# A mixture-of-experts kernel: the experts' multiplications in whole fp32 on row halves of TensorE, instead of high and low parts

## The chip, the cores and the metric

One core of a Trainium2 chip runs the kernel. The metric is the time of one execution in device microseconds (us); three runs of the kernel before gave 1051.89, 1052.32 and 1053.75 us, median 1052.32. Everything is fp32 on the outside.

## What is computed

The input x is 64 images of 64 channels and 16x16 pixels. First comes a normalisation over the channels, two quantised 3x3 convolutions with batch normalisation, and residual sums. The result is read as 16384 tokens of 64 channels, and each token goes through its best two of eight experts:

```python
logits = flat @ router_w.T
topk_probs, topk_idx = jax.lax.top_k(jax.nn.softmax(logits, axis=-1), 2)
gates = ...                                   # the two probabilities, normalised to a sum of 1
h1 = jnp.einsum('nc,ehc->neh', flat, w1)      # c = 64, h = 682
h3 = jnp.einsum('nc,ehc->neh', flat, w3)
y = jnp.einsum('neh,ech->nec', silu(h1) * h3, w2)
out = jnp.einsum('ne,nec->nc', gates, y)
```

The kernel computes only the two experts that a token is sent to: 32768 rows of 64 numbers.

## The kernel before, in words

**Stages.** Normalisation and the first convolution (to about 124 us of the span), then the second convolution with the routing (to about 265), then the experts, 68 tiles of up to 512 rows (to about 996), then the gated sum of each token's two results and the store. Each engine has its own program; order between them comes from semaphores alone.

**Routing, in eight pairs of stripes** (`pairs`, `route`). A stripe is 1024 tokens. For each pair, VectorE finds the two experts and the place of each token's row in a DRAM table `expert_rows` in which every expert has a region. GpSimd (POOL) copies a stripe's rows and places into its own buffers (`stage`, lines 556 and 557) and writes them to the table by 16 indirect DMAs of 128 rows (line 563). In `route(p)` the weights of expert p are also made ready: VectorE splits them into a high part (rounded to fp32r) and a low part (`high`, `low`, lines 970 to 983), TensorE turns eleven blocks of 128x128 (`stack_weights`, line 1341) and six pieces of w2 (lines 1348, 1349), ScalarE copies them out of PSUM (lines 702 to 707), and SyncE (SP) writes them to DRAM. `stack_weights(p)` stands on TensorE ahead of the transposes and logits of the next pair and of the position sums of this one.

**Tiles.** A tile is 512 rows of one expert; 56 of them (NF) are full, the other 12 hold 256 rows each of two experts ("two"). `tiles` gives the order on all engines. Per tile:
- SP loads the rows (`load_rows`) and the weights (`load_weights`: w1 and w3 stacked, 704 KB, and w2, 192 KB), two tiles ahead, when the buffers of the tile two before are free.
- VectorE `split` (lines 1126 to 1145): where each result row goes, and the rows' high and low parts side by side in `hl`.
- TensorE `turn` (line 1384): four transposes to PSUM; ScalarE `copy_xT` (lines 732 to 735) copies them to two tiles, [high; low] and [low; high] over the 128 partitions, in three instructions.
- TensorE `up` (line 1405): the 682 hidden columns are six blocks (KT), five of 128 and one of 42. A block takes two fp32r multiplications for h1 and two for h3, each over all 128 rows of the array (64 channels, high and low). In the last block the 42 columns of h1 and the 42 of h3 lie in one stationary tile. That makes 22 multiplications of 512 columns in a full tile.
- ScalarE `silu` (line 726), VectorE `hidden` (line 1157, the product), with PSUM banks in threes.
- TensorE `down` (line 1420): whole fp32 multiplications, whose stationary operand is 64 columns wide. Blocks k and k+1 go to the two column halves of the array: `y_ps[h:h + 64]`, h = 0 or 64. The last block has 42 rows. A whole fp32 multiplication leaves two records in the trace, an fp32r one leaves one.
- ScalarE `copy_y` (line 740), TensorE `rows_out` (line 1432, four transposes), VectorE `rows_out` (lines 1164 and 1165), and POOL `scatter_y` (line 583): four indirect DMAs of 128 rows into `result_rows`.

**What orders the work around it.** TensorE's tile j is written out by hand: turn(j+1), up 2, up 3, down 0, up 4, rows_out(j-1), up 5, down 2, up 0 and up 1 of tile j+1, down 4. VectorE's `rows_out(j)` waits until POOL's results of tile j-2 are stored (`y_out`), since there are two buffers. POOL's own order is fixed too:

```python
            def four_tiles(j, s, u):
                stage(s, u)
                for i in range(4):
                    scatter(u, i // 2, range(i % 2 * G, i % 2 * G + G))
                    scatter_y(j + i, i % 2)
```

So POOL writes six stripes alone, then one of the other ten stripes per four tiles: in tiles 0 to 39 it issues four indirect DMAs of rows and four of results per tile. In tiles 40 to 47 it issues two of pad rows (line 594) and four of results, in tiles 48 to 67 four of results alone.

Of the kernel before, what the change touches and what calls it, by code (L numbers as in the profile page):

```python
# [15 lines left out]
ALU = mybir.AluOpType  # L16
# [13 lines left out]
def conv_moe_kernel(nc, x, gamma1, beta1, w1, gamma2, beta2, w2, pat, router_w, ew1, ew2, ew3, out):  # L30
# [29 lines left out]
    WST = (2 * HT + 1) * 128  # L60
    LV = len(SNAPS)
    TAIL3 = 64
# [9 lines left out]
    with ExitStack() as ctx:  # L72
# [90 lines left out]
        wr = sb("w13_rows", [128, 2, HT, C])  # L163
        wt = sb("w13_tail", [128, C])
        wr2 = sb("w2_rows", [C, HID])
        wsp = sb("w13_split", [128, 2 * HT + 1, 2, C], F32R)
        wstk = sb("w13_stacked", [128, WST], F32R)
# [3 lines left out]
        wbuf = [[sb(f"w13_{u}", [128, WST], F32R)[:, :] for u in range(2)]]  # L171
# [3 lines left out]
        wbuf.append([wsp[:, :, :, :].rearrange("p t d c -> p (t d c)"), wstk[:, :]])  # L175
# [20 lines left out]
        hbuf = [carve(T) for u in range(4)]  # L196
# [5 lines left out]
        xT = [[sb(f"xT_{p}_{u}", [128, T], F32R) for u in range(2)] for p in ("hi_lo", "lo_hi")]  # L202
# [55 lines left out]
        w_zero = sem("w_zeroed")  # L258
        ws_rdy = sem("w_split_ready")
# [111 lines left out]
        def _(sp):  # L371
# [21 lines left out]
            sp.wait_ge(w_zero, 1)  # L393
            def weights_in(e):
                for k, w in enumerate((ew1, ew3)):
                    we = w.rearrange("e h c -> e (h c)")
                    sp.dma_start(wr[:, k, :, :].rearrange("p t c -> p (t c)"),
                                 we[bass.ds(e, 1), 0:HT * 128 * C].rearrange("a (p n) -> (a p) n", p=128)
                                 ).then_inc(w_in, 16)
                    sp.dma_start(wt[TAIL3 * k:TAIL3 * k + HR, :],  # L400
                                 we[bass.ds(e, 1), HT * 128 * C:HID * C].rearrange("a (p n) -> (a p) n", p=HR)
                                 ).then_inc(w_in, 16)
# [4 lines left out]
            def weights_out(e):  # L407
                sp.dma_start(wsc[bass.ds(e * 128, 128), :], wstk[:].bitcast(F32)).then_inc(w_out, 16)
# [4 lines left out]
            with sp.Fori(0, E - 1) as e:  # L413
                sp.wait_ge(ws_rdy, 2 * e + 2)
                weights_in(e + 1)
                sp.wait_ge(wt_sb, 4 * e + 4)
                weights2_in(e + 1)
                weights_out(e)
            sp.wait_ge(wt_sb, 4 * E)
# [21 lines left out]
            def load_weights(j, u, two=0, first=False):  # L441
                for i in range(1 + two):
                    at = tmap[0:1, 2 + two, bass.ds(2 * j - 2 * NF + i if two else j, 1)]
                    exp = sp.value_load(at, min_val=0, max_val=(E - 1) * 128)
                    if not first and i == 0:
                        sp.wait_ge(h1_rdy, KT * j - KT)
                    sp.dma_start(wbuf[i][u].bitcast(F32), wsc[bass.ds(exp, 128), :]).then_inc(wt_in[i][u], 16)
# [193 lines left out]
        def _(act):  # L641
# [48 lines left out]
            def route(p, first=False, last=0):  # L690
# [8 lines left out]
                for b in range(3):  # L699
                    n = min(512, WST - 512 * b)  # L700
                    act.wait_ge(wt_ps, 4 * p + b + 1)
                    nc.scalar.activation(wstk[:, 512 * b:512 * b + n], w_bank(b)[:, 0:n],
                                         ACT.Copy).then_inc(wt_sb, 1)
                act.wait_ge(wt_ps, 4 * p + 4)
                nc.scalar.activation(w2s[:, 0:HT, :].rearrange("p k c -> p (k c)"), w_bank(3)[:, 0:HT * C],
                                     ACT.Copy)
                nc.scalar.activation(w2s[0:HR, HT, :], w_bank(3)[0:HR, HT * C:KT * C],
# [20 lines left out]
            def copy_xT(j, u, part):  # L728

                if part == 0:  # L730
                    act.wait_ge(xt_rdy, j + 1)
                    nc.scalar.activation(xT[0][u][:], turn_ps[:], ACT.Copy)  # L732
                    nc.scalar.activation(xT[1][u][0:C, :], turn_ps[C:2 * C, :], ACT.Copy)  # L733
                else:
                    nc.scalar.activation(xT[1][u][C:2 * C, :], turn_ps[0:C, :], ACT.Copy).then_inc(xt_sb, 1)  # L735
# [6 lines left out]
            def tile(j, u, two, first=False, last=0):  # L742
                if not first:
                    copy_y(j - 1, 1 - u)
                if last != 1:
                    copy_xT(j + 1, 1 - u, 0)
                silu(j, 2)
                if last != 1:
                    copy_xT(j + 1, 1 - u, 1)
                for k in range(3, KT):  # L750
                    silu(j, k)
                if last != 1:
                    silu(j + 1, 0)
                    silu(j + 1, 1)

            copy_xT(0, 0, 0)
            copy_xT(0, 0, 1)
            silu(0, 0)
            silu(0, 1)
# [15 lines left out]
        def _(dve):  # L775
# [34 lines left out]
            V.memset(wt[:], 0.0)  # L810
            V.memset(w2s[:], 0.0).then_inc(w_zero, 1)
# [63 lines left out]
            pipelined(dve, spread, norm, NP)  # L875

# [86 lines left out]
            def route(p, first=False, last=0):  # L963
                c = r_chain.begin(p, 21)
                wideof = lambda a, n: a.unsqueeze(2).broadcast_to([128, a.shape[1], n])
                wr_ = wr[:].rearrange("p k t c -> p (k t) c")
# [3 lines left out]

                def high():
                    dve.wait_ge(w_in, 64 * p + 64)
                    V.tensor_copy(wsp[:, 0:2 * HT, 0, :], wr_)
                    V.tensor_copy(wsp[:, 2 * HT, 0, :], wt[:]).then_inc(ws_rdy, 1)

                def low(n):
                    def work():
                        dve.wait_ge(ws_rdy, 2 * p + 1)
                        a = slice(4 * n, min(4 * n + 4, 2 * HT))
                        ins = V.tensor_tensor(wsp[:, a, 1, :], wr_[:, a], wsp[:, a, 0, :].bitcast(F32), ALU.subtract)  # L980
                        if 4 * n + 4 >= 2 * HT:
                            V.tensor_tensor(wsp[:, 2 * HT, 1, :], wt[:], wsp[:, 2 * HT, 0, :].bitcast(F32), ALU.subtract
                                            ).then_inc(ws_rdy, 1)
                    return work
# [14 lines left out]
                assert 2 * HT <= 12  # L999

# [492 lines left out]
```

## Time and profile before

| | us |
|---|---|
| median of three runs | 1052.32 |
| runs | 1051.89 to 1053.75 |
| span of the profiled execution | 1053.6 |
| TensorE busy / VectorE / ScalarE / POOL | 932.6 / 627.8 / 500.6 / 611.6 |
| first `up` to the end of the last tile | 269.7 to about 996 |

The span runs from the first to the last instruction; no other time of the profiled execution is shown, and the span is 1.3 us over the median. Busy means that at least one instruction of the engine was under way. Ends of multiplications are modelled and overlap, so TensorE can look busy throughout while it streams less than it could; the distance from one start to the next is the better measure. PE is TensorE's multiplication, PEld its load of the stationary operand, DVE VectorE, ACT ScalarE.

### The profile page before, as it was taken

To read this page: it belongs to the slowest core of one execution; us is meant where nothing else is said; L and a number is where in the kernel's file an instruction comes from. 1 tells how busy PE (TensorE), PEld (TensorE's weight loads), DVE (VectorE), ACT (ScalarE), POOL (GpSimd) and SP (SyncE) were. 2 spreads that over 40 slices of the span, in tenths; PEclk is the share of its full clock that TensorE was granted. 3 is DMA by queue.
4 is the path that set the end of the run, shared out by engine and by line. 5 is a ranking of instruction groups with operands and counts; after the bars stand their busy time and mean duration, and the time that the engine had idled before them with its cause. 6 is when DMAs were issued, how large, how long until landed. Compare 5 with 4: busy or idle time off the path is not lost.

```text
span 1053.6 us, 18732 instructions
## 1 busy us (share of the span) xinstructions
PE 932.6 (89%) x4463; PEld 542.0 (51%) x4463; DVE 627.8 (60%) x1475; ACT 500.6 (48%) x858; POOL 611.6 (58%) x649
## 2 busy tenths in 40 slices
PE   4968798882899999999999999999999999999723
PEld 2753266651455555555454545454545467777512
DVE  3775589798555555555555555555555555555457
ACT  3214444332456565656565656565656565555300
POOL 3640017777777777777777777776653333434452
PEclk9888899795799999999999999999999999999955
DMA  7100023342343444443434343434343356565177
GB/s 171 23 1 1 0 73 127 130 135 90 125 132 118 133 118 132 118 133 117 134 117 134 117 131 119 131 119 128 111 126 105 120 166 195 170 197 182 50 246 233
DMA packets 72237, 129.24 MB, mean 123 GB/s; under 512 B 15861, under 2 KB 47790, under 8 KB 72208
## 3 DMA queue, kind: packets, MB, share of 16 engines
q1 hardware_dynamic: 50448, 107.10, 33.4%
q0 software_dynamic: 17408, 17.62, 5.0%
q10 hardware_dynamic: 4352, 4.20, 1.5%
q8 instruction: 11, 0.18, 0.1%
q14 instruction: 18, 0.15, 0.0%
HBM read 99.67 MB, written 29.71 MB: 123 GB/s over the span
## 4 chain that ended last, share of the span: by engine, by line
PE 77%; DVE 11%; issue 5%; DMA 2%; ACT 1%; SPq 1%; POOL 1%; DVEq 1%; ACTq 0%; POOLq 0%
PE bank L1405 35%; PE bank L1420 26%; PE bank L1384 4%; PE bank L1307 3%; PE bank L1432 3%; PE bank L1321 1%; PE bank L1258 1%; PE bank L1326 1%; DMA y_and_rows<-expert_w 1%; DVE stats L1003 1%; PE bank L1242 1%; DMA y_and_rows<-result_rows 1%; DVE y_and_rows L1203 1%; PE bank L1247 1%; ACT quant_tmp L666 1%
## 5 line engine op out<-in xcount | busy, mean ns | idle before, releaser
L1157 DVE TENSOR_TENSOR conv_all<-conv_all,bank 128x512 f32<-128x512 f32 (+1 forms) x408 | 280.6, 688 | 319.2 <-PE bank L1405 165.4
L583 POOL DMA_INDIRECT result_rows<-conv_all,dest_now x272 | 272.1, 1000 | 199.4 <-DVE conv_all L1165 122.5
L726 ACT ACTIVATE conv_all<-bank 128x512 f32<-128x512 f32 (+1 forms) x408 | 243.6, 597 | 186.8 <-PE bank L1405 184.3
L1405 PE MATMUL bank<-xT_hi_lo,w 128*128 128x512 f32 (+1 forms) x748 | 307.1, 411 | 2.4 <-issue 1.9
L563 POOL DMA_INDIRECT expert_rows<-rows_now,slot_now x256 | 248.1, 969 | 86.5 <-issue 68.9
L1405 PE MATMUL bank<-xT_lo_hi,w 128*128 128x512 f32 (+1 forms) x748 | 280.7, 375 | 0.0
L1420 PE MATMUL bank<-conv_all,w 128*64 128x512 f32 (+3 forms) x816 | 267.1, 579 | 0.5 <-DVE conv_all L1157 0.5
L1405 PEld LDWEIGHTS bank<-xT_hi_lo,w 128*128 128x128 f32 x748 | 141.6, 189 | 120.8 <-DVE conv_all L1157 90.6
L1405 PEld LDWEIGHTS bank<-xT_lo_hi,w 128*128 128x128 f32 x748 | 141.9, 190 | 17.3
L1420 PEld LDWEIGHTS bank<-conv_all,w 128*64 128x64 f32 (+1 forms) x816 | 52.7, 134 | 116.6 <-issue 111.8
L740 ACT ACTIVATE conv_all<-bank 128x512 f32<-128x512 f32 x68 | 40.6, 597 | 132.1 <-PE bank L1420 132.1
L1307 PE MATMUL bank<-quant_padded,conv_w_blocks 128*128 128x512 bf16 x288 | 75.2, 415 | 11.0 <-DVE quant_padded L922 6.5
L556 POOL COPY rows_now<-y_and_rows 128x528 f32 (+1 forms) x16 | 10.7, 666 | 77.9 <-DVE slot_all L1036 77.9
L1384 PEld LDWEIGHTS bank<-ident,conv_all 128*128 128x128 f32 x272 | 29.2, 143 | 51.6 <-issue 48.7
L1307 PEld LDWEIGHTS bank<-quant_padded,conv_w_blocks 128*128 128x128 bf16 x288 | 27.7, 102 | 54.3 <-issue 22.1
L732 ACT ACTIVATE xT_hi_lo<-bank 128x512 fp32r<-128x512 f32 x68 | 40.7, 599 | 18.5 <-PE bank L1384 18.5
L1463 PE MATMUL bank<-ident,y_and_rows 128*128 128x128 f32 x64 | 14.8, 408 | 36.9 <-DVE y_and_rows L1214 36.9
L1384 PE MATMUL bank<-ident,conv_all 128*128 128x128 f32 x272 | 45.4, 290 | 1.8 <-DVE conv_all L1144 1.8
L1165 DVE TENSOR_REDUCE conv_all<-bank 128x256 f32<-128x512 f32 x68 | 46.4, 683 | 0.0
L1432 PE MATMUL bank<-ident,conv_all 128*128 128x128 f32 x272 | 40.8, 272 | 0.7 <-ACT conv_all L740 0.7
L733 ACT ACTIVATE xT_lo_hi<-bank 64x512 fp32r<-64x512 f32 x68 | 40.5, 596 | 0.8
L735 ACT ACTIVATE xT_lo_hi<-bank 64x512 fp32r<-64x512 f32 x68 | 40.1, 589 | 1.7
(247 smaller groups left out, 975.0 us busy)
## 6 DMA issues: line engine op xcount, KB each, us to landing
w<-expert_w SPq DMA_DIRECT2D x68, 704.0 KB, 4.2
w<-expert_w SPq DMA_DIRECT2D x68, 192.0 KB, 2.4
y_and_rows<-result_rows SPq DMA_DIRECT2D x16, 512.0 KB, 6.5
conv_all<-expert_rows SPq DMA_DIRECT2D x56, 132.0 KB
expert_w<-w_stacked SPq DMA_DIRECT2D x8, 704.0 KB
result_rows<-conv_all,dest_now POOLq DMA_INDIRECT x272
w_split<-expert_w SPq DMA_DIRECT2D x6, 704.0 KB, 4.2
w_stacked<-expert_w SPq DMA_DIRECT2D x6, 704.0 KB, 4.1
```

The costliest lines, as they stand in the source:

```text
L563: nc.gpsimd.indirect_dma_start(xs, bass.IndirectOffsetOnAxis(ap=slot[u][:, k * GH + g:k * GH + g + 1], axis=0), rows[u][:, g * ROW:g * ROW ...
L583: nc.gpsimd.indirect_dma_start(yout, bass.IndirectOffsetOnAxis(ap=destc[u][:, g:g + 1], axis=0), yrow[u][:, g, :], None, bounds_check=2 * ...
L726: nc.scalar.activation(sbuf[k % 3][0:m, :], h1_ps[k % 3][0:m, :], ACT.Silu).then_inc(silu_rdy, 1)
L732: nc.scalar.activation(xT[0][u][:], turn_ps[:], ACT.Copy)
L740: nc.scalar.activation(ysb[u], y_ps[:], ACT.Copy).then_inc(y_sb, 1)
L1157: V.tensor_tensor(hbuf[(2 * u + k) % 4][0:m, :], sbuf[k % 3][0:m, :], h3, ALU.mult).then_inc(mul_rdy, 1)
L1165: V.tensor_reduce(yrow[u], turn_ps[:].rearrange("p (g h c) -> p g c h", g=4, h=2), AX.X, ALU.add).then_inc(yr_sb, 1)
L1307: ins = mm(conv_ps[u][:], wblk[:, l, t, :], qpad[u][:, :, ky:ky + H, kx:kx + W], start=t == 0, stop=t == TAPS - 1)
L1384: ins = nc.tensor.transpose(turn_ps[:, 128 * g:128 * g + 128], hl[u][:, g, :, :].rearrange("p d c -> p (d c)"), ident[:])
L1405: ins = mm(ps[k % 3][:, rows_], wbuf[i][u][:, 128 * c:128 * c + 128], xT[p][u][:, rows_], start=p == 0, stop=p == 1)
L1420: ins = mm(y_ps[h:h + 64, rows_], w2buf[e][u][0:m, i, :], hbuf[(2 * u + i) % 4][0:m, rows_], start=i < 2 and e == 0, stop=i >= KT - 2 and ...
L1432: ins = nc.tensor.transpose(turn_ps[:, 128 * g:128 * g + 128], ysb[u][:, 128 * g:128 * g + 128], ident[:])
```

## The change

Experts' up multiplications take whole fp32 operands. w1 and w3 of a block stand one over the other on the 128 partitions: partitions 0 to 63 hold the 64 channels of w1, partitions 64 to 127 those of w3, and the turned rows `xT` are the same 64 channels twice. h1 uses the upper 64 rows of the array, h3 the lower 64, each into its own PSUM bank. The last block is a pair like the others, and `down` takes it with 128 rows, of which the rows past 42 of the weights and of the hidden values are zeros. The split into high and low is gone for weights and rows (VectorE copies the rows twice into `hl` instead, and ScalarE's `copy_xT` is one instruction). The weights for a load shrink to 768 columns (384 KB). The order of a tile becomes up 0 to 5 (with rows_out(j-1) after up 2), turn(j+1), down 0, 2, 4; VectorE and ScalarE follow that order.

```diff
-    WST = (2 * HT + 1) * 128
+    WST = KT * 128
...
-        hbuf = [carve(T) for u in range(4)]
+        hbuf = [carve(T) for k in range(HT)] + [wide[:].rearrange("p g c -> p (g c)")[:, 0:T]]
...
-        xT = [[sb(f"xT_{p}_{u}", [128, T], F32R) for u in range(2)] for p in ("hi_lo", "lo_hi")]
+        xT = [sb(f"xT_{u}", [128, T]) for u in range(2)]
...
@@ ScalarE, tile @@
             def tile(j, u, two, first=False, last=0):
                 if not first:
                     copy_y(j - 1, 1 - u)
-                if last != 1:
-                    copy_xT(j + 1, 1 - u, 0)
-                silu(j, 2)
-                if last != 1:
-                    copy_xT(j + 1, 1 - u, 1)
-                for k in range(3, KT):
+                for k in range(KT):
                     silu(j, k)
                 if last != 1:
-                    silu(j + 1, 0)
-                    silu(j + 1, 1)
+                    copy_xT(j + 1, 1 - u)
...
@@ VectorE, route @@
-                high()
                 dve.wait_ge(rsd_rdy, 2 * p + 2)
-                rstd(c, low(0), low(1), low(2))
+                rstd(c)
...
@@ VectorE, split @@
-                c(V.tensor_copy(hl[u][:, :, 0, :].bitcast(F32R), xr))
-                V.tensor_tensor(hl[u][:, :, 1, :], xr, hl[u][:, :, 0, :], ALU.subtract).then_inc(split_rdy, 1)
+                V.tensor_copy(hl[u], xr.unsqueeze(2).broadcast_to([128, 4, 2, C])).then_inc(split_rdy, 1)
...
@@ VectorE, tile @@
+                for k in range(KT):
+                    hidden(j, u, k)
+                    if k == 1 and not first:
+                        rows_out(j - 1, 1 - u)
                 if not last:
                     split(j + 2, u, two[2])
-                for k in range(2, KT):
-                    hidden(j, u, k)
-                    if k == 4 and not first:
-                        rows_out(j - 1, 1 - u)
-                if last != 1:
-                    hidden(j + 1, 1 - u, 0)
-                    hidden(j + 1, 1 - u, 1)
...
@@ TensorE, stack_weights @@
-                pe.wait_ge(ws_rdy, 2 * p + 2)
-                for b in range(3):
-                    if b == 2:
-                        pe.wait_ge(wt_sb, 4 * p + 1)
-                    for t in range(4 * b, min(4 * b + 4, 2 * HT + 1)):
-                        ins = nc.tensor.transpose(w_bank(b)[:, 128 * (t % 4):128 * (t % 4) + 128],
-                                                  wsp[:, t, :, :].bitcast(F32).rearrange("p d c -> p (d c)"), ident[:])
+                pe.wait_ge(w_in, 64 * p + 64)
+                for t in range(HT):
+                    ins = nc.tensor.transpose(w_bank(t // 4)[:, 128 * (t % 4):128 * (t % 4) + 128], wr[:, t, :, :].rearrange("p k c -> p (k c)"), ident[:])
+                nc.tensor.transpose(w_bank(1)[:, 128:128 + HR], wt[:].rearrange("p k c -> p (k c)"),
+                                    ident[0:HR, 0:HR]).then_inc(wt_ps, 1)
...
@@ TensorE, up @@
-                if k < HT:
-                    parts = ((h1_ps, k, h1_rdy), (h3_ps, HT + k, h3_rdy))
-                else:
-                    parts = ((h1_ps, 2 * HT, h1_rdy),)
-                for ps, c, rdy in parts:
-                    for i in range(1 + two):
-                        rows_ = slice(TH * i, TH * i + (T >> two))
-                        for p in range(2):
-                            ins = mm(ps[k % 3][:, rows_], wbuf[i][u][:, 128 * c:128 * c + 128], xT[p][u][:, rows_],
-                                     start=p == 0, stop=p == 1)
-                    ins.then_inc(rdy, 1)
+                for i in range(1 + two):
+                    rows_ = slice(TH * i, TH * i + (T >> two))
+                    for ps, h, rdy in ((h1_ps, 0, h1_rdy), (h3_ps, C, h3_rdy)):
+                        ins = mm(ps[k % 3][:, rows_], wbuf[i][u][h:h + C, 128 * k:128 * k + 128], xT[u][h:h + C, rows_],
+                                 start=True, stop=True)
+                        if i == two:
+                            ins.then_inc(rdy, 1)
...
@@ TensorE, down @@
-                        m = 128 if i < HT else HR
                         h = 64 * (i % 2)
-                        ins = mm(y_ps[h:h + 64, rows_], w2buf[e][u][0:m, i, :], hbuf[(2 * u + i) % 4][0:m, rows_],
+                        ins = mm(y_ps[h:h + 64, rows_], w2buf[e][u][:, i, :], hbuf[i][:, rows_],
...
@@ TensorE, tile @@
+                for k in range(KT):
+                    up(j, u, k, two[0])
+                    if k == 2 and not first:
+                        rows_out(j - 1, 1 - u)
                 if last != 1:
                     turn(j + 1, 1 - u, first)
-                up(j, u, 2, two[0])
-                up(j, u, 3, two[0])
-                down(j, u, 0, two[0])
-                up(j, u, 4, two[0])
-                if not first:
-                    rows_out(j - 1, 1 - u, last == 1)
-                up(j, u, 5, two[0])
-                down(j, u, 2, two[0])
-                if last != 1:
-                    up(j + 1, 1 - u, 0, two[1])
-                    up(j + 1, 1 - u, 1, two[1])
-                down(j, u, 4, two[0])
+                for k in range(0, KT, 2):
+                    down(j, u, k, two[0])
```

POOL's program is not touched. The loads of w1 and w3 from their inputs go to a layout with 64 columns of w1 and 64 of w3 side by side, in pieces of 256 bytes.

## Rows read from the trace of the kernel before

**Rows 1.** The page, section 1 (engine, busy, instructions), and the windows (last: PEclk, DMA, GB/s).
```profile
PE 932.6 (89%) x4463; PEld 542.0 (51%) x4463; DVE 627.8 (60%) x1475; ACT 500.6 (48%) x858; POOL 611.6 (58%) x649
...
285.00:711.00 426.00, 426.00 (x1699) 220.84 (x1698) 233.65 (x483) 241.09 (x406) 321.50 (x339) 1.00 0.41 125
```

**Rows 2.** Timeline, VectorE: `rows_out` of tiles 0, 41, 49, 55, 66 and 67.
```profile
289.25 0.68 DVE L1165 TENSOR_REDUCE conv_all<-bank 128x256 f32<-128x512 f32 x1
...
722.12 0.68 DVE L1165 TENSOR_REDUCE conv_all<-bank 128x256 f32<-128x512 f32 x1
...
806.55 0.68 DVE L1165 TENSOR_REDUCE conv_all<-bank 128x256 f32<-128x512 f32 x1
...
869.98 0.68 DVE L1165 TENSOR_REDUCE conv_all<-bank 128x256 f32<-128x512 f32 x1
...
990.62 0.68 DVE L1165 TENSOR_REDUCE conv_all<-bank 128x256 f32<-128x512 f32 x1
996.07 0.69 DVE L1165 TENSOR_REDUCE conv_all<-bank 128x256 f32<-128x512 f32 x1
```

**Rows 3.** Timeline, POOL: first DMAs of tiles 0, 4, 8; last of tile 39; tiles 40, 41.
```profile
284.74 0.98 POOL L563 DMA_INDIRECT expert_rows<-rows_now,slot_now  x1 [0.82 <-POOL slot_now L557]
...
290.82 1.00 POOL L583 DMA_INDIRECT result_rows<-conv_all,dest_now  x1 [1.30 <-DVE conv_all L1165]
...
329.14 0.98 POOL L563 DMA_INDIRECT expert_rows<-rows_now,slot_now  x1 [0.83 <-POOL slot_now L557]
...
371.71 0.99 POOL L563 DMA_INDIRECT expert_rows<-rows_now,slot_now  x1 [0.84 <-POOL slot_now L557]
...
709.36 0.98 POOL L583 DMA_INDIRECT result_rows<-conv_all,dest_now  x1 [0.30 <-issue]
...
714.66 1.00 POOL L583 DMA_INDIRECT result_rows<-conv_all,dest_now  x1 [0.30 <-issue]
...
723.92 1.00 POOL L583 DMA_INDIRECT result_rows<-conv_all,dest_now  x1 [0.30 <-issue]
```

**Rows 4.** Timeline, PE: one full tile's column pair (first look at 500.3), ups, last pair.
```profile
500.26 0.65 PE L1420 MATMUL bank<-conv_all,w 128*64 128x512 f32 x2
...
500.26 1.08 PE L1420 MATMUL bank<-conv_all,w 128*64 128x512 f32 x4
501.27 0.50 PE L1405 MATMUL bank<-xT_hi_lo,w 128*128 128x512 f32 x1
501.61 0.39 PE L1405 MATMUL bank<-xT_lo_hi,w 128*128 128x512 f32 x1
501.84 0.40 PE L1405 MATMUL bank<-xT_hi_lo,w 128*128 128x512 f32 x1
...
503.33 2.07 PE L1420 MATMUL bank<-conv_all,w 128*64 128x512 f32 x4
505.34 0.66 PE L1384 MATMUL bank<-ident,conv_all 128*128 128x128 f32 x4
```

**Rows 5.** Groups by form: `down` records, product and silu of one block.
```profile
L1157 DVE TENSOR_TENSOR conv_all<-conv_all,bank 128x512 f32<-128x512 f32 x340 | 233.7, 687 | 316.8 <-PE bank L1405 165.4 <-ACT conv_all L726 148.9 <-PE bank L1420 2.6
L726 ACT ACTIVATE conv_all<-bank 128x512 f32<-128x512 f32 x340 | 203.4, 598 | 135.1 <-PE bank L1405 132.6
L1420 PE MATMUL bank<-conv_all,w 128*64 128x512 f32 x560 | 180.9, 618 | 0.0
```

**Rows 6.** Timeline, PE: the last `down` of a half tile, and the transposes behind it.
```profile
906.43 1.22 PE L1420 MATMUL bank<-conv_all,w 128*64 128x256 f32 x4
907.58 1.22 PE L1420 MATMUL bank<-conv_all,y_and_rows 128*64 128x256 f32 x4
908.73 0.66 PE L1384 MATMUL bank<-ident,conv_all 128*128 128x128 f32 x4
```

**Rows 7.** Routing: the transposes of `stack_weights` that go (timeline), POOL's first work.
```profile
144.05 0.55 PE L1341 MATMUL bank<-ident,w_split 128*128 128x128 f32 x3 [0.25 <-ACT w_stacked L702]
...
151.43 0.62 POOL L556 COPY rows_now<-y_and_rows 128x528 f32<-128x528 f32 x1 [77.91 <-DVE slot_all L1036]
```

**Rows 8.** DMA issues (KB each, us to landing): an indirect DMA of 128 rows; the weights' load.
```profile
w<-expert_w SPq DMA_DIRECT2D x68, 704.0 KB, 4.2
...
expert_rows<-pad_rows,pad_now POOLq DMA_INDIRECT x16, 2.5
```

More of the change, by code:

```diff
@@ L160, in conv_moe_kernel @@
         pads = [sb(f"pad_now{u}", [128, 1], I32) for u in range(2)]
-        wr = sb("w13_rows", [128, 2, HT, C])
-        wt = sb("w13_tail", [128, C])
+        wr = sb("w13_rows", [128, HT, 2, C])
+        wt = sb("w13_tail", [HR, 2, C])
         wr2 = sb("w2_rows", [C, HID])
-        wsp = sb("w13_split", [128, 2 * HT + 1, 2, C], F32R)
-        wstk = sb("w13_stacked", [128, WST], F32R)
+        wstk = sb("w13_stacked", [128, WST])
         w2s = sb("w2_stacked", [128, KT, C])
-        wbuf = [[sb(f"w13_{u}", [128, WST], F32R)[:, :] for u in range(2)]]
+        wbuf = [[sb(f"w13_{u}", [128, WST])[:, :] for u in range(2)]]
         w2buf = [[sb(f"w2_{u}", [128, KT, C])[:, :, :] for u in range(2)]]
-        wbuf.append([wsp[:, :, :, :].rearrange("p t d c -> p (t d c)"), wstk[:, :]])
+        wbuf.append([sb("w13_second", [128, WST])[:, :], wstk[:, :]])
         w2buf.append([yb[:, u * KT * C:(u + 1) * KT * C].rearrange("p (k c) -> p k c", k=KT) for u in range(2)])
@@ L698, in route @@
                     wait_apart(act, w_out, 32 * p)
-                for b in range(3):
-                    n = min(512, WST - 512 * b)
-                    act.wait_ge(wt_ps, 4 * p + b + 1)
+                for b in range(2):
+                    n = min(512, HID - 512 * b)
+                    act.wait_ge(wt_ps, 3 * p + b + 1)
                     nc.scalar.activation(wstk[:, 512 * b:512 * b + n], w_bank(b)[:, 0:n],
                                          ACT.Copy).then_inc(wt_sb, 1)
-                act.wait_ge(wt_ps, 4 * p + 4)
-                nc.scalar.activation(w2s[:, 0:HT, :].rearrange("p k c -> p (k c)"), w_bank(3)[:, 0:HT * C],
+                act.wait_ge(wt_ps, 3 * p + 3)
+                nc.scalar.activation(w2s[:, 0:HT, :].rearrange("p k c -> p (k c)"), w_bank(2)[:, 0:HT * C],
                                      ACT.Copy)
-                nc.scalar.activation(w2s[0:HR, HT, :], w_bank(3)[0:HR, HT * C:KT * C],
+                nc.scalar.activation(w2s[0:HR, HT, :], w_bank(2)[0:HR, HT * C:KT * C],
                                      ACT.Copy).then_inc(wt_sb, 1)
@@ L726, in silu, with copy_xT @@
                 nc.scalar.activation(sbuf[k % 3][0:m, :], h1_ps[k % 3][0:m, :], ACT.Silu).then_inc(silu_rdy, 1)
[L728 to L733, printed above, removed]
-                else:
-                    nc.scalar.activation(xT[1][u][C:2 * C, :], turn_ps[0:C, :], ACT.Copy).then_inc(xt_sb, 1)
+            def copy_xT(j, u):
+                act.wait_ge(xt_rdy, j + 1)
+                nc.scalar.activation(xT[u][:], turn_ps[:], ACT.Copy).then_inc(xt_sb, 1)
             def copy_y(j, u):
@@ L744, in tile @@
                     copy_y(j - 1, 1 - u)
[L745 to L750 removed]
+                for k in range(KT):
                     silu(j, k)
                 if last != 1:
[L753 to L759 removed]
+                    copy_xT(j + 1, 1 - u)
+            copy_xT(0, 0)
             tiles(act, tile)
@@ L807, in _ @@
                 dve.sem_inc(s_, 1)
[L810 to L811 removed]
+            V.memset(w2s[:], 0.0)
+            V.memset(wstk[:], 0.0)
             V.memset(run[:], 0.0)
```

72 lines of the change are left out of this document (24 added, 48 removed).

## The prediction

> **What bounds the kernel now.** I read the page first, then the windows, then one tile on TensorE, then POOL. The page has TensorE busy 89% of the span, and in the 426 us from 285 to 711 us it is busy throughout at a granted clock of 1.00 (its 2.4 GHz level), while POOL is busy 321.5 us there [rows 1]. VectorE's reductions in `rows_out` mark the tiles: from tile 0 (289.25) to tile 41 (722.12) a tile takes 432.87/41 = 10.56 us; from 49 to 55, 63.43/6 = 10.57; in half tiles, 55 to 66, 120.64/11 = 10.97 [rows 2]. The pace is the same early and late, so TensorE sets it.
>
> POOL has hardly more air, though, and its busy share hides that. Four tiles of its fixed order, from 329.14 to 371.71, take 42.57 us, or 10.64 per tile: 32 indirect DMAs of about 0.98 us with 0.30 us of issue before each, and a stage [rows 3]. That is slightly slower than TensorE. POOL falls behind from tile to tile: its results of tile 39 end at 709.36 + 0.98 = 710.3, and it uses the lighter tiles from 40 on (723.92 - 714.66 = 9.26 us each) to catch up [rows 3]. TensorE is held nowhere only because POOL may be two tiles late. So there are two limits within 1% of each other in tiles 0 to 39, and the change touches one of them.
>
> **The change, part by part.** The sum is made on the span, 1053.6 us, and carried over to the median, 1052.3.
>
> *Down, last block.* A column pair starts at 500.26 and what follows it at 501.27: 1.01 us for two whole fp32 multiplications, whose first records are both under way in a look of 0.3 us. The last pair, 128 rows against 42, takes 503.33 to 505.34 = 2.01: one after the other [rows 4]. Padded, it is a pair. How much does a pair cost without the change of shape before it? A record of `down` lasts 618 ns in the mean [rows 5]; an fp32r multiplication lasts 0.39 while the next starts after 0.23 (501.61, 501.84) [rows 4], so some 0.16 is tail, a whole fp32 record streams 0.43 to 0.46, and a pair of two records 0.86 to 0.92. I take 0.86. The block goes from 2.01 to 0.86: -1.15. In a half tile 906.43 to 908.73 = 2.30 becomes 0.86: -1.44 [rows 6].
>
> *Up.* 22 fp32r multiplications at 0.23, 5.1 us, become six pairs at 0.86, 5.16, if the row halves run side by side as the column halves do: +0.1. In whole fp32 an operand costs twice the columns' time, and stacking two weights wins it back. The chief gain is not here.
>
> *Changes of shape.* The eight ups from 501.27 to 503.33 take 2.06 against 8 x 0.23 = 1.84 [rows 4], and a pair 1.01 against 0.86: about 0.17 per change of shape. The order before has six apart from the one in the last pair, the new one five (ups, rows_out, ups, turn, down, ups): -0.17.
>
> *The chain up, silu, product.* The last record of a block starts 0.43 after the block and lasts 0.6; silu takes 0.60, the product 0.69 [rows 5], with about 0.2 for semaphores: 2.5 to 2.7 us until the bank is free, against three blocks of 0.86 = 2.58. The transposes between up 2 and up 3 give that chain 0.4 more. VectorE's `rows_out` (0.84) now stands between products 1 and 2, so up 5 may come some 0.1 late: +0.1. Its `split` stands at the tile's end, where nothing waits for it until the next tile's turn, and `down 4` has about 0.6 us after product 5. ScalarE loses two copies of 0.6.
>
> So TensorE's tile becomes 10.56 - 1.15 + 0.1 - 0.17 + 0.1 = 9.4; I take 9.5. A half tile: 10.97 - 1.44 - 0.17 + 0.1 + 0.1 = 9.6; there records are half as long and each still brings a load of 128 columns, so I take 9.8, and 10.5 as the bad end.
>
> *What POOL lets through.* In tiles 0 to 39 the limit is now POOL's 10.64. `rows_out(j)` on VectorE waits until the results of j-2 are stored, product 2 stands behind it, and up 5 and the next turn behind that. What POOL gains: tile 0's results waited 1.30 us for VectorE and the first four tiles took 329.14 - 284.74 = 44.4 against 42.57 [rows 3]: -1.8. TensorE's new tile 0 with `rows_out` early in tile 1 comes in time even if the start stays. And POOL's first work at 151.43 waits for the first places; ahead of their sums TensorE gives up the third bank of weights, 0.55 us [rows 7]: -0.6 (0 to -2; VectorE's splits go too, but TensorE is the later). Thus POOL's tile 39 ends at 710.3 - 2.4 = 707.9; an indirect DMA lands 2.5 us after its start [rows 8], so `rows_out(41)` can run at 709.4 + 0.2 = 709.6 instead of 722.12 [rows 2]: **-12.5**. That is the whole gain of the first 42 tiles, and all of it is the two tiles that TensorE can be ahead of POOL.
>
> *Tiles 41 to 49.* POOL's 9.26 is under 9.5, so TensorE sets the pace: 8 x 9.5 = 76.0 against 84.4: **-8.4**.
> *Tiles 49 to 55.* 57.0 against 63.4: **-6.4**.
> *Half tiles 55 to 66.* 107.8 against 120.6: **-12.8**.
> *The end.* From `rows_out(66)` to `rows_out(67)` it was 5.45 [rows 2]; now three ups, three downs, copy_y (0.6) and the transposes lie between, some 7.2: **+1.8**.
>
> Sum -38.3. The closing stage is untouched. The loads of a tile shrink from 704 to 384 KB [rows 8], were not waited for, and give nothing. The inputs' loads in pieces of 256 bytes have a routing pair, over 10 us, to land. Prediction: 1052.3 - 38.3 = 1014.
>
> **The rivals.**
>
> *Weight loads that don't hide.* The four transposes from 505.34 show that loads of 128 columns follow each other at some 0.11 us or a little more [rows 4]. In `down` the loads are of 64 columns and hide. Were each record of a row half to pay its 128-column load, a block would cost 0.22 more: 1.3 per tile, 10.8, slower than POOL and than before. Full tiles 55 x 0.24 = +13; half tiles, with four records per half in turn, 2.6 more, 12.4: 11 x 1.43 = +16; the end +2.5. About 1084. For it: no row here has a 128-column load in a half of the array. Against: in the full array they hide under 0.23. The Trainium skill ("TensorE: Matmul & The Clock Gate", Part 3, what overlaps and what doesn't) says that a load overlaps running multiplications only when its row group differs. By that rule the second record of a half would wait for its own half's first, which is this rival; the trace of before does not agree for the whole array. Chance 8%.
>
> *The row halves take turns.* This is the slower side's main case. If h1 and h3 are not side by side, a block costs 1.72, a tile 9.5 + 5.2 = 14.7, a half tile 15.0. From tile 0 to 55: 55 x 4.14 = +228; 55 to 66: 11 x 4.03 = +44; first tile and end +10: about 1334. It decides as soon as a block costs over 1.05 us, since 6 x 0.19 takes the tile to POOL's and the old pace. For it: pairs of unlike row counts do run in turn in the last `down` [rows 4], and no row shows row halves. Against: equal column halves run together in whole fp32. Chance 9%.
>
> *A slower chain.* Block after block through ScalarE and VectorE at 2.9 us instead of 2.6, or pairs at 0.95: tiles of 10.2 and 10.6. Then only the 12.5 stays whole, with 3 + 2 + 4 - 2 from the rest: about 1033. Chance 8%.
>
> *POOL is no limit.* Then 55 tiles save 1.06 each and the half tiles 12.8 less 1.8: about -69, 983. Its DMAs leave one another 0.30 us in every row; only cheaper DMAs could do it. Chance 3%.
>
> **The numbers.** Forecast 72%. It spans a start of routing 0 to 2 us earlier, full tiles of 9.3 to 9.9 and half tiles of 9.5 to 10.5: 1005 to 1027. The range reaches to the slower chain and somewhat past it: 1004 to 1042. The slower side is the first two rivals, 17%, with 1% more for a chain at the old pace; within 0.2% (2 us, about what a measurement of this kernel can tell from no change) 1%; faster 81%.
>
> **What would show it.** `rows_out` of tiles 3 to 40 at 10.64 us apart, and POOL without a wait on VectorE from 152 to 780 us; `rows_out(41)` near 710; from there 9.5 us per tile and 9.8 in half tiles. On TensorE the records of h1 and h3 start within some 10 ns of each other, 0.43 after the pair before; the last `down` pair takes as long as the others; gaps appear before up 5 or turn in tiles 4 to 40. Records of h1 and h3 0.43 or more apart, or a mean of 10.7 in the last tiles, would prove it wrong.

## The result: 4% faster, and the profile after

| | before | after |
|---|---|---|
| median of four runs beside each other | 1053.03 | 1012.29 |
| lowest to highest | 1051.89 to 1054.07 | 1010.43 to 1014.12 |
| profiled execution: its time, span | 1053.6 (span) | 1013.82, 1011.7 |

The ratio is 0.9605, interval 0.9582 to 0.9629; the forecast was 1014. All times are in us.

The page of the kernel after: busy time of each engine, against [rows 1]; the chain of work that ended last, by engine; the ups and VectorE's copy at the head of `rows_out` (busy, mean ns of one, idle time before them and what ended it); and one line of its waits from 320 to 700 us (total, times, longest).

```profile
PE 862.1 (85%) x4583; PEld 432.3 (43%) x4583; DVE 591.1 (58%) x1360; ACT 413.7 (41%) x714; POOL 609.9 (60%) x649
...
PE 43%; POOL 23%; issue 17%; DVE 11%; DMA 2%; ACT 2%; SPq 1%; POOLq 1%; DVEq 1%; ACTq 0%
...
L1357 PE MATMUL bank<-xT,w 64*128 64x512 f32 (+1 forms) x1632 | 376.0, 576 | 26.8 <-DVE conv_all L1117 25.9
...
L1124 DVE COPY dest_now<-dest_all 128x4 int32 (+1 forms) x68 | 12.2, 179 | 59.4 <-DMA result_rows<-conv_all,dest_now 46.5
```
```profile
DVE dest_now L1124 <- DMA result_rows<-conv_all,dest_now: 44.8, 32, 2.4
```

TensorE, 932.6 before, is busy 70 us less; POOL keeps its 610 and now holds 23% of the chain. VectorE waits 44.8 us in that stretch for a results' DMA, and TensorE 25.9 in the ups for VectorE's products. The bound has moved from TensorE to POOL in the first stage of the tiles, up to tile 41.

The timeline after, VectorE's `rows_out` of tiles 0, 41, 49, 55, 66, 67, against [rows 2]:

```profile
284.37 0.68 DVE L1125 TENSOR_REDUCE conv_all<-bank 128x256 f32<-128x512 f32 x1
...
708.44 0.68 DVE L1125 TENSOR_REDUCE conv_all<-bank 128x256 f32<-128x512 f32 x1
...
784.56 0.68 DVE L1125 TENSOR_REDUCE conv_all<-bank 128x256 f32<-128x512 f32 x1
...
841.35 0.69 DVE L1125 TENSOR_REDUCE conv_all<-bank 128x256 f32<-128x512 f32 x1
...
945.66 0.69 DVE L1125 TENSOR_REDUCE conv_all<-bank 128x256 f32<-128x512 f32 x1
952.54 0.69 DVE L1125 TENSOR_REDUCE conv_all<-bank 128x256 f32<-128x512 f32 x1
```

| stretch | before | after | gained | forecast |
|---|---|---|---|---|
| start to `rows_out(41)` | 722.12 | 708.44 | 13.7 | 12.5 |
| tiles 41 to 49 | 84.43 | 76.12 | 8.3 | 8.4 |
| 49 to 55 | 63.43 | 56.79 | 6.6 | 6.4 |
| half tiles 55 to 66 | 120.64 | 104.31 | 16.3 | 12.8 |
| 66 to 67 | 5.45 | 6.88 | -1.4 | -1.8 |
| from there to the end | 57.5 | 59.2 | -1.6 | 0 |

The gains add up to 41.9, the difference of the two spans. A full tile takes 56.79/6 = 9.47, a half tile 104.31/11 = 9.48.

POOL after, against [rows 3]: first row DMAs of tiles 0, 4 and 8, the first results' DMA, and the last of tile 39.

```profile
285.37 0.98 POOL L558 DMA_INDIRECT expert_rows<-rows_now,slot_now  x1 [0.82 <-POOL slot_now L552]
...
290.52 1.00 POOL L578 DMA_INDIRECT result_rows<-conv_all,dest_now  x1 [0.30 <-issue]
...
328.03 0.98 POOL L558 DMA_INDIRECT expert_rows<-rows_now,slot_now  x1 [0.83 <-POOL slot_now L552]
...
370.50 0.98 POOL L558 DMA_INDIRECT expert_rows<-rows_now,slot_now  x1 [0.84 <-POOL slot_now L552]
...
705.98 0.98 POOL L578 DMA_INDIRECT result_rows<-conv_all,dest_now  x1 [0.30 <-issue]
```

Its wait for VectorE at tile 0 is gone (1.30 before; now 0.30 of "issue", time in which the engine waits for nothing that the profile shows), and its four tiles take 370.50 - 328.03 = 42.47, as before. It ends tile 39 at 706.96, and `rows_out(41)` runs 1.5 later: TensorE can be two tiles ahead of POOL's results, no more.

One full tile on TensorE after, against [rows 4]; then a look 0.3 us wide at its first ups; then VectorE beside it.

```profile
482.27 2.85 PE L1357 MATMUL bank<-xT,w 64*128 64x512 f32 x12
485.05 0.66 PE L1384 MATMUL bank<-ident,conv_all 128*128 128x128 f32 x4
485.63 1.99 PE L1357 MATMUL bank<-xT,w 64*128 64x512 f32 x8
488.09 1.13 PE L1357 MATMUL bank<-xT,w 64*128 64x512 f32 x4 [0.47 <-DVE conv_all L1117]
489.15 0.66 PE L1341 MATMUL bank<-ident,conv_all 128*128 128x128 f32 x4
```
```profile
482.27 0.70 PE L1357 MATMUL bank<-xT,w 64*128 64x512 f32 x2
```
```profile
486.67 0.17 DVE L1124 COPY dest_now<-dest_all 128x4 int32 x1 [1.07 <-DMA result_rows<-conv_all,dest_now]
486.75 0.68 DVE L1125 TENSOR_REDUCE conv_all<-bank 128x256 f32<-128x512 f32 x1
487.35 1.87 DVE L1117 TENSOR_TENSOR conv_all<-conv_all,bank 128x512 f32<-128x512 f32 x3
```

Three blocks, twelve records, take 485.05 - 482.27 = 2.78, a block 0.93. The look finds two records under way, by the program's order one of h1 and one of h3. The chain of POOL's limit is all here: VectorE waits 1.07 for stored results, the products stand behind it, and up 5 starts 0.47 late.

### The profile page after: what moved, and what is told of

The parts are those of the page before. It is cut to its first block, busy times and chain, and to the rows that moved or that the text cites. A ratio compares the mean times of both kernels' runs of the same rounds, so it can differ in the third digit from the quotient of the medians.

```text
span 1011.7 us, 18515 instructions
## 1 busy us (share of the span) xinstructions
PE 862.1 (85%) x4583; PEld 432.3 (43%) x4583; DVE 591.1 (58%) x1360; ACT 413.7 (41%) x714; POOL 609.9 (60%) x649
## 4 chain that ended last, share of the span: by engine, by line
PE 43%; POOL 23%; issue 17%; DVE 11%; DMA 2%; ACT 2%; SPq 1%; POOLq 1%; DVEq 1%; ACTq 0%
PE bank L1357 18%; POOL result_rows L578 12%; POOL expert_rows L558 10%; PE bank L1372 9%; PE bank L1263 3%; PE bank L1277 2%; PE bank L1341 2%; PE bank L1384 2%; PE bank L1282 2%; PE bank L1214 1%; DMA result_rows<-conv_all,dest_now 1%; DVE stats L968 1%; DMA y_and_rows<-result_rows 1%; PE bank L1198 1%; PE bank L1203 1%
## 5 line engine op out<-in xcount | busy, mean ns | idle before, releaser
L1357 PE MATMUL bank<-xT,w 64*128 64x512 f32 (+1 forms) x1632 | 376.0, 576 | 26.8 <-DVE conv_all L1117 25.9
L1117 DVE TENSOR_TENSOR conv_all<-conv_all,bank 128x512 f32<-128x512 f32 x340 | 227.2, 684 | 226.1 <-ACT conv_all L721 218.4
L1357 PEld LDWEIGHTS bank<-xT,w 64*128 64x128 f32 x1632 | 142.1, 187 | 212.4 <-issue 131.4
L1372 PE MATMUL bank<-conv_all,w 128*64 128x512 f32 (+1 forms) x680 | 179.8, 569 | 0.0
L1372 PEld LDWEIGHTS bank<-conv_all,w 128*64 128x64 f32 x680 | 52.0, 137 | 80.2 <-issue 76.7
L1372 PE MATMUL bank<-rstd_wide,w 128*64 128x512 f32 (+1 forms) x136 | 64.3, 554 | 0.0
L1117 DVE TENSOR_TENSOR rstd_wide<-conv_all,bank 42x512 f32<-42x512 f32 x68 | 46.2, 680 | 24.8 <-ACT conv_all L721 22.4
L551 POOL COPY rows_now<-y_and_rows 128x528 f32 (+1 forms) x16 | 10.5, 656 | 77.3 <-DVE slot_all L1000 77.3
L1341 PEld LDWEIGHTS bank<-ident,conv_all 128*128 128x128 f32 x272 | 28.9, 142 | 47.8 <-issue 46.1
L1384 PEld LDWEIGHTS bank<-ident,conv_all 128*128 128x128 f32 x272 | 28.4, 140 | 46.8 <-issue 45.7
L726 ACT ACTIVATE xT<-bank 128x512 f32<-128x512 f32 x68 | 40.6, 597 | 17.2 <-PE bank L1341 17.0
L1124 DVE COPY dest_now<-dest_all 128x4 int32 (+1 forms) x68 | 12.2, 179 | 59.4 <-DMA result_rows<-conv_all,dest_now 46.5
```

The lines of the kernel that those rows point to most:

```text
L726: nc.scalar.activation(xT[u][:], turn_ps[:], ACT.Copy).then_inc(xt_sb, 1)
L1117: V.tensor_tensor(hbuf[k][0:m, :], sbuf[k % 3][0:m, :], h3, ALU.mult).then_inc(mul_rdy, 1)
L1341: ins = nc.tensor.transpose(turn_ps[:, 128 * g:128 * g + 128], hl[u][:, g, :, :].rearrange("p d c -> p (d c)"), ident[:])
L1357: ins = mm(ps[k % 3][:, rows_], wbuf[i][u][h:h + C, 128 * k:128 * k + 128], xT[u][h:h + C, rows_], start=True, stop=True)
L1372: ins = mm(y_ps[h:h + 64, rows_], w2buf[e][u][:, i, :], hbuf[i][:, rows_], start=i < 2 and e == 0, stop=i >= KT - 2 and e == two)
L1384: ins = nc.tensor.transpose(turn_ps[:, 128 * g:128 * g + 128], ysb[u][:, 128 * g:128 * g + 128], ident[:])
```

## The experiments

The runs fell on several chips. On two of them, called disturbed below, the kernel before took 1296 to 1319 instead of 1053 (last section). Each ratio is against the kernel before on the same chip. On a disturbed chip only tiles 49 to 55 are compared, where full tiles go within 0.12 of their normal pace. Half tiles there are longer in some of the runs: 11.05 in the kernel with padding alone (9.76 undisturbed), 9.99 with four buffers (9.52), 9.88 with eight (9.49).

The change itself ran a second time, on the undisturbed chip on which the padding alone and both kernels with four buffers ran too: 1011.95 (1011.31 to 1012.50) against 1053.56, ratio 0.9608 (0.9572 to 0.9643), with full tiles of 9.47 and half tiles of 9.48 again.

**Padding alone.** The kernel before with the last block of `down` taking 128 rows; run on both sorts of chip.

```diff
-                        m = 128 if i < HT else HR
-                        ins = mm(y_ps[h:h + 64, rows_], w2buf[e][u][0:m, i, :], hbuf[(2 * u + i) % 4][0:m, rows_],
+                        ins = mm(y_ps[h:h + 64, rows_], w2buf[e][u][:, i, :], hbuf[(2 * u + i) % 4][:, rows_],
```

> The kernel before with one edit: the last block of down takes all 128 rows (the weights' rows past 42 are zeros). High and low parts, 22 ups and the old order stay. Theory A (the padding is the gain; whole fp32 on row halves is worth nothing by itself): a full tile becomes 10.56 - 1.15 = 9.4 us where POOL lets it, a half tile 10.97 - 1.44 = 9.5, tiles 3 to 40 run at POOL's 10.6, and the time is about 1053 - 44 = 1009 us, as fast as the change or a little faster. Theory B (the row halves and the new order carry a good part of the gain): the tile stays over 9.9 us after tile 42 and the time over 1025.

On a disturbed chip: 1291.06 against 1308.85, ratio 0.9847 (0.9789 to 0.9904). Tiles 49 to 55 take 9.70 each there, half tiles 11.05; this run alone looked like theory B.

> The kernel before with the last block of down padded, a second time, since the first run was held up by late instructions. Theory A: 9.4 us per full tile after tile 42, 9.5 per half tile, 1009 us where instructions arrive in time, the same as the change within 5 us. Theory B: half tiles of over 10.5 us, as in the first run, and a time over 1025: then the halves of high and low parts, with 44 loads of 128 columns and 704 KB of weights each, are themselves dearer in half tiles than whole fp32.

On an undisturbed chip 1018.36 against 1053.56, ratio 0.9672 (0.9636 to 0.9708). `rows_out` of tiles 41, 49, 55, 66, 67, and then the last pair of a full tile with what follows it:

```profile
708.76 0.68 DVE L1165 TENSOR_REDUCE conv_all<-bank 128x256 f32<-128x512 f32 x1
...
783.99 0.68 DVE L1165 TENSOR_REDUCE conv_all<-bank 128x256 f32<-128x512 f32 x1
...
841.47 0.68 DVE L1165 TENSOR_REDUCE conv_all<-bank 128x256 f32<-128x512 f32 x1
...
948.79 0.68 DVE L1165 TENSOR_REDUCE conv_all<-bank 128x256 f32<-128x512 f32 x1
952.99 0.69 DVE L1165 TENSOR_REDUCE conv_all<-bank 128x256 f32<-128x512 f32 x1
```
```profile
815.54 1.08 PE L1419 MATMUL bank<-conv_all,w 128*64 128x512 f32 x4
816.55 0.66 PE L1384 MATMUL bank<-ident,conv_all 128*128 128x128 f32 x4
```

A full tile takes 57.48/6 = 9.58, a half tile 107.32/11 = 9.76, the end 4.20. The padding saves 0.99 of the 1.10 in a full tile and 1.21 of the 1.49 in a half tile. The pair itself went from 2.01 [rows 4] to 816.55 - 815.54 = 1.01. Two half tiles took 10.45 and 10.21; most of the others took about 9.67, which is 1.28 less than the usual 10.95 before. `rows_out(41)` is at 708.76, 0.3 behind the change's: at POOL's limit every faster tile gives the same.

So padding alone brings 35.2 of the 41.6 that the change brings on this chip (from 1053.56 to 1018.36, against 1011.95). Neither theory is met: 1018 lies between 1009 and 1025, because a full tile is 9.58 and not 9.4, a half tile 9.76 and not 9.5.

**The change without the padding**, run twice, both times on a disturbed chip.

```diff
+                        m = 128 if i < HT else HR
-                        ins = mm(y_ps[h:h + 64, rows_], w2buf[e][u][:, i, :], hbuf[i][:, rows_],
+                        ins = mm(y_ps[h:h + 64, rows_], w2buf[e][u][0:m, i, :], hbuf[i][0:m, rows_],
```

> The changed kernel with the last block of down back at 42 rows of the operands. Theory A: the last pair takes 2.0 instead of 0.86 us, a full tile 9.47 + 1.15 = 10.6, a half tile 9.5 + 1.4 = 10.9; that is POOL's pace, so nearly all of the gain is gone: about 1012 + 8 + 10 + 9 + 16 = 1053, between 1045 and 1056. Theory B: most of the gain stays, under 1030.

> The changed kernel with the last block of down at 42 rows again, a second time, on a chip where instructions arrive in time. Tiles of 10.45 (as in the first run's tiles 42 to 52) and half tiles of 10.79, so tiles 0 to 39 are at POOL's pace of 10.56 with TensorE almost level with it: rows_out of tile 41 near 716 us, the end 25 to 30 us behind the change, total 1040 to 1052, ratio 0.99 to 1.00. If padding were not the main thing it would stay under 1030.

1282.34, ratio 0.9807 (0.9741 to 0.9873); the second time 1283.86, 0.9812 (0.9765 to 0.9859). Tiles 49, 55, 66 of the first:

```profile
1032.59 0.69 DVE L1125 TENSOR_REDUCE conv_all<-bank 128x256 f32<-128x512 f32 x1
...
1095.35 0.69 DVE L1125 TENSOR_REDUCE conv_all<-bank 128x256 f32<-128x512 f32 x1
...
1213.80 0.68 DVE L1125 TENSOR_REDUCE conv_all<-bank 128x256 f32<-128x512 f32 x1
```

62.76/6 = 10.46, and in half tiles 118.45/11 = 10.77; the second run has the same paces. Against the change (9.47, 9.48) the padding is worth 0.99 and 1.29 in the new order too, and against the kernel before (10.57, 10.97) row halves with the new order bring 0.1 and 0.2. These are differences between chips. The half tiles could be disturbed here, but both runs agree within 0.01 per tile, and in the old order the last pair of a half tile went from 2.30 [rows 6] to 1.01, also 1.29. The whole time and the forecast of 1040 to 1056 were not tested, as the stages before tile 41 are disturbed.

**Both ups on one row half.** h3 is computed from w1 on the upper 64 rows, so its values are not those of the reference; the number of multiplications is the same.

```diff
-                    for ps, h, rdy in ((h1_ps, 0, h1_rdy), (h3_ps, C, h3_rdy)):
+                    for ps, h, rdy in ((h1_ps, 0, h1_rdy), (h3_ps, 0, h3_rdy)):
```

> The changed kernel with h1 and h3 both on the upper 64 rows of the array; h3 is then made from w1 instead of w3, so the output is another function. The number of records, columns and loads is the same. Theory A (the halves run side by side because their rows differ): records of h1 and h3 come one after the other, a block costs 1.72 us, a tile 9.47 + 5.2 = 14.6, and the time is 1012 + 38 x 4.1 + 27 x 5.2 + 6, about 1320 us. Rival (records of one matmul overlap whatever their rows): 1012.

1435.14 (one run, on a disturbed chip; its tile 0 comes at 400.8 instead of 284.4, which is what it is over the forecast of 1320), tiles 49 and 55, and three blocks of ups with what follows:

```profile
1116.02 0.68 DVE L1125 TENSOR_REDUCE conv_all<-bank 128x256 f32<-128x512 f32 x1
...
1203.56 0.68 DVE L1125 TENSOR_REDUCE conv_all<-bank 128x256 f32<-128x512 f32 x1
```
```profile
1101.02 5.41 PE L1357 MATMUL bank<-xT,w 64*128 64x512 f32 x12
1106.36 0.66 PE L1341 MATMUL bank<-ident,conv_all 128*128 128x128 f32 x4
```

87.54/6 = 14.59 against 9.47, +5.1; the same twelve records take 5.34 instead of 2.78. Tiles 3 to 39 take 14.60 each as well, with TensorE busy 509.9 of the 510 us from 390 on, so the disturbance does not touch this pace. This is the rival in which row halves take turns, made to happen: its price of 5.2 per tile is right, and the change does not pay it. Row halves that run side by side are what makes whole fp32 affordable.

**More result buffers.** The theory says that TensorE is two tiles ahead of POOL because `y_rows` has two buffers; a slower TensorE would not react to more. First four, then eight, with one semaphore each. The edit of eight, cut to its core (the loops of VectorE and POOL are written out in groups of eight to match):

```diff
-        yrow = [carve(4, C) for u in range(2)]
+        yrow = [sb(f"y_rows{u}", [128, 4, C])[:, :, :] for u in range(8)]
-        y_out = [sem(f"y_scatter{u}") for u in range(2)]
+        y_out = [sem(f"y_scatter{u}") for u in range(8)]
...
-                    scatter_y(j + i, i % 2)
+                    scatter_y(j + i, w + i)
```

> The changed kernel with four result buffers instead of two, so that VectorE may be four tiles ahead of POOL's stores. Theory A (POOL is the limit of tiles 3 to 40 and the two buffers are how it holds TensorE): rows_out of tile 43 instead of 41 runs at about 708 us, all later tiles some 19 us earlier, POOL's own times unchanged up to 707, total about 993. Rival (something else, such as row loads or the stripes' order, holds tiles 3 to 40): no change, 1012.

> The changed kernel with four result buffers, a second time. Theory A: rows_out of tile 43 at about 708 us, total about 993 where instructions arrive in time; on a chip with late instructions about 0.975 of the kernel before, as in the first run. Rival: 1012.

On a disturbed chip 1275.74 against 1308.85, ratio 0.9746 (0.9694 to 0.9798), which decides nothing. On the undisturbed one 997.71 against 1053.56, ratio 0.9476 (0.9441 to 0.9511). Its tiles 41, 55, 67, and its wait from 320 to 700 us:

```profile
689.96 0.68 DVE L1125 TENSOR_REDUCE conv_all<-bank 128x256 f32<-128x512 f32 x1
...
824.14 0.69 DVE L1125 TENSOR_REDUCE conv_all<-bank 128x256 f32<-128x512 f32 x1
...
935.74 0.68 DVE L1125 TENSOR_REDUCE conv_all<-bank 128x256 f32<-128x512 f32 x1
```
```profile
DVE dest_now L1124 <- DMA result_rows<-conv_all,dest_now: 18.8, 13, 3.8
```

Tile 41 comes 18.5 earlier (17.6 against the second run of the change) with POOL's program as long as before; the wait shrinks from 44.8 to 18.8. The total is 4.7 over the forecast of 993: of the 17.6 at tile 41, 16.3 are left in the span, and 14.2 in the medians.

**Four buffers with the padding alone**, in the kernel before:

> The kernel before with the padded last block and four result buffers, high and low parts kept. Theory A: both limits move as in the changed kernel with four buffers, rows_out of tile 43 at about 710 us, later tiles at 9.4, the last tile 2.6 us shorter than the change's, total about 990. Theory B: over 1005, because half tiles with two loads of 704 KB and 44 loads of 128 columns stay near 10.5.

999.09 (997.75 to 1001.06), ratio 0.9494 (0.9457 to 0.9531); tile 41 at 691.85. It is 9 over theory A's 990: full tiles take 9.57 and half tiles 9.61, where 9.4 was expected. The medians of the two kernels with four buffers differ by 1.4 (997.71, range 996.22 to 998.12), and the ranges overlap: with four buffers no gain from the row halves is shown. With two buffers the change was 6.4 faster than the padding alone (1011.95 against 1018.36), of which half tiles are 107.32 - 104.33 = 3.0; the rest was not traced to one cause.

**Eight buffers.**

> The changed kernel with eight result buffers. Theory A: TensorE, at 9.47 us per tile, runs freely from the first tile to the last, since POOL falls behind by 39 x (10.56 - 9.47) = 43 us, under five tiles, until tile 39 and then catches up; rows_out of tile 67 near 284.4 + 66 x 9.48 + 6.9 = 917 us instead of 952, total about 977 (0.928 of the kernel before), POOL still without a pause until about 780. Rival (with four buffers already the rest is something else, row loads or the stripes): as with four buffers, 0.948, 998.

> The changed kernel with eight result buffers, a second time. Where instructions arrive in time, Theory A: rows_out of tile 67 near 917 to 922 us, total about 977 to 982, ratio 0.93, below the four buffers' 0.948. Rival: 998. On the chip with late instructions: 0.964, as in the first run, which decides nothing.

On a disturbed chip 1261.0 against 1305.66, ratio 0.9642 (0.9605 to 0.9678). On an undisturbed one 981.04 (979.53 to 982.45, six runs) against 1054.9, ratio 0.9302 (0.9278 to 0.9326): the fastest version here, which beats the change too. Its tiles 0, 41, 55, 67, POOL's last DMA of tile 39, and one row of TensorE:

```profile
280.36 0.68 DVE L1126 TENSOR_REDUCE y_rows<-bank 128x256 f32<-128x512 f32 x1
...
671.11 0.69 DVE L1126 TENSOR_REDUCE y_rows<-bank 128x256 f32<-128x512 f32 x1
...
810.34 0.68 DVE L1126 TENSOR_REDUCE y_rows<-bank 128x256 f32<-128x512 f32 x1
...
921.63 0.68 DVE L1126 TENSOR_REDUCE y_rows<-bank 128x256 f32<-128x512 f32 x1
```
```profile
707.87 0.98 POOL L578 DMA_INDIRECT result_rows<-y_rows,dest_now  x1 [0.30 <-issue]
```
```profile
709.74 5.18 PE L1367 MATMUL bank<-xT,w 64*128 64x512 f32 x12 [4.45 <-DMA w<-expert_w]
```

POOL ends tile 39 at 708.85, as late as ever, while 41 tiles take 390.75/41 = 9.53 each, TensorE's own pace. The wait of the results is gone from the list. One new wait is left: TensorE stands 4.45 us once, for a tile whose loads went out at 708.9, after POOL's last stripes of rows. The twelve records after it take 5.18 instead of 2.85; the granted clock was 0.77 from 705 to 710 us, 0.50 from 710 to 712 and 0.59 from 712 to 715, after 1.00. So the one wait costs 6.8: that tile took 16.24. That POOL's rows are what the loads waited for is argued from the order, not tested.

**Less for POOL.** The change with three of four groups of results stored; the last quarter of the results is left a copy of x, written by two plain DMAs.

```diff
-                for g in range(4):
+                for g in range(3):
```

> The changed kernel with two result buffers, but POOL stores only three of the four groups of 128 result rows of each tile (the fourth quarter of the results is left at a copy of x, made early by two plain DMAs on SP's queue). POOL's tile is then 10.56 - 1.29 = 9.27 us in tiles 0 to 39, below TensorE's 9.47. Theory A: all tiles at 9.47, rows_out of tile 67 near 917 us and a span of about 975. Rival (POOL is not what holds tiles 3 to 40): 1010.

It fell on a disturbed chip: 1206.43 in its one run, where the change without the padding took 1284 and eight buffers 1261; the change itself was not run on such a chip. From tile 3 to tile 39 it takes 12.8 per tile, against 14.0 and 13.9 for those two, although their own TensorE paces differ by 1 us. From 42 on it runs at 9.47. That fewer of POOL's DMAs help is suggested by this one run; the expected number could not show, since this stage ran at neither engine's normal pace.

## Why the prediction was right

**The bound and where it moves.** Right. `rows_out(41)` fell to 708.44 where 709.6 was forecast, and more buffers, with POOL's program no shorter, brought it to 690 and 671. POOL's pace of 10.64 was a little too slow: the four tiles shown take 10.62 each, and over tiles 8 to 36 the mean is 10.56 against 10.63 before, as its indirect DMAs from 360 to 660 us last 975 ns in the mean and not 984. Over the tiles up to 39 that is some 2.6 us, against a miss of 1.4 the other way at the start (next paragraph); the 1.2 between forecast and measurement at tile 41 is what the two errors leave. The limit also did not bind from tile 3 on: tiles 1 to 8 took 9.2 to 9.7 each, TensorE's own pace, and POOL held it from tile 9 on. That changes nothing at tile 41.

**The start.** -1.8 for POOL's waits came as said. From the second convolution's start to POOL's first DMA it took 23.16 against 24.93, a gain of 1.8 where 0.6 was forecast; in the other undisturbed traces with the change's routing it was 1.8, 0.9 and 0.6, and the kernel before with padding alone, whose routing is the old one, shows 0.5. So the forecast's term is neither confirmed nor refuted. But that start came at 130.83 against 128.27, at a granted clock of 0.76 between 80 and 100 us against 0.84, so POOL began at 153.99, after the 153.20 of before. The first convolution is not part of the change, and with eight buffers the clock there was 0.84 again. POOL's start was forecast 0.6 earlier and came 0.8 later.

**The tile.** 9.5 was forecast and 9.47 measured: the mechanism was right, and the closeness is luck, since two errors cancel. The padding was forecast at -1.15 and is -0.99 in both orders: the lone pair of 2.01 was laid against 0.86, but in the old order a pair in its place still pays a change of shape and takes 1.01, as the other column pairs of [rows 4] did. The row for that was there. In the new order the padded pair takes 0.96 and the unpadded one 1.95. Ups and order were forecast at +0.03 together and are -0.1. A block of ups is 0.93 with its share of the change of shape.

**The half tile.** The term that was mis-sized: forecast 9.8, measured 9.48, 3.5 us over eleven tiles. The padding gave 1.21 to 1.29 instead of 1.44. Ups, order and loads together were forecast at +0.23 (+0.03, and 0.2 for loads of 128 columns) and are 10.77 - 10.97 = -0.2. The rows of the ups show no cost for the loads:

```profile
880.35 0.60 PE L1357 MATMUL bank<-xT,w_second 64*128 64x256 f32 x4
880.78 0.62 PE L1357 MATMUL bank<-xT,w 64*128 64x256 f32 x4
881.23 0.60 PE L1357 MATMUL bank<-xT,w_second 64*128 64x256 f32 x4
```

Four records of 256 columns, two on each row half, take 0.43 to 0.45, as long as two of 512 columns side by side, and the trace has as many loads as records on this line. The forecast said that the Trainium skill ("TensorE: Matmul & The Clock Gate", Part 3, what overlaps and what doesn't) lets a load run beside multiplications of another row group only. The runs disagree with that sentence for this case: with records 0.22 apart on each half, each half's loads were hidden as well.

**The rivals.** Row halves taking turns: refuted by 9.47, and shown to cost 5.1 when forced. Loads that don't hide: refuted, as just said. The slower chain: up 5 waits in tiles 9 to 40, but for POOL through VectorE; after tile 41 the tile is 9.47. POOL as no limit: refuted by the waits and by the buffers, which moved tile 41 while POOL's program stayed.

**The end.** 6.88 against 7.2 forecast. The closing stage, whose code is the same, took 1.6 more, at a granted clock of 0.53 against 0.54; it lasts 57.5 to 61.1 in the undisturbed traces of this case, and no cause was looked for.

**What the traces were to show.** Records of h1 and h3 started within 7 ns of each other, pairs 0.43 apart, as said. From tile 9 on `rows_out` is not evenly 10.6 apart but 11.5, 10.27, 10.18, 10.28 in turn, with POOL's group of four tiles.

## What to carry to other kernels

Where two engines have nearly the same pace, cost a change on the one by how far it may run ahead of the other: here a tile of 1.1 us less, 41 times, gave 13.7, and a ring of eight result buffers in place of two gave back 31 more. Count the pace of an issuing engine from one repeat of its order, not from its busy share. Test the parts of a change one by one: here the padding, the smallest edit, carried 35 of the 42. And price a padded or paired operation against its neighbour in the same place, which pays for the change of shape too.

## What had not been expected of the hardware

That loads of 128 columns hide in both row halves even with records of 256 columns, 0.22 apart: half tiles took 9.48, about as long as full ones. And that the change of shape is paid by a column pair of equal row counts too: the padded pair saved 0.99, not 1.15. That a pair of 128 and 42 rows runs in turn and a pair of 128 and 128 side by side is all that is shown; pairs of other counts were not run.

On two chips the same kernels took some 1.25 times as long (before: 1306 and 1309 against 1053 in the medians). Most of the time is lost up to about 940 us: in the change without the padding tile 0 comes at 386 instead of 284 us, and tiles 3 to 39 take 13.9 each instead of some 10.5. In the routing stage TensorE's rows there read like these, of that kernel:

```profile
166.48 0.20 PE L1318 MATMUL bank<-chosen,ones_bf 128*128 128x48 bf16 x1 [1.24 <-issue]
167.91 0.19 PE L1318 MATMUL bank<-chosen,ones_bf 128*128 128x40 bf16 x1 [1.23 <-issue]
```

TensorE waits for nothing that the profile shows, over a microsecond before each of these instructions, and with POOL's DMAs of rows gone full tiles reach their normal pace again; half tiles stayed longer in three of the six kernels run there. The one run with fewer POOL DMAs had shorter tiles, which fits instructions that come late beside them; the cause was not settled. Padding alone, four and eight buffers stand in the same order on both sorts of chip, with about half the gain on the disturbed ones (ratios 0.985, 0.975, 0.964 against 0.967, 0.948, 0.930).
